# A fused cross-attention and quantised feed-forward kernel: the last up maximum by bank, first tiles in halves, even conversions two ahead

## The reference, cut to what matters

```python
def act_qdq(x):                       # 16 bits, one scale for the whole tensor
    scale = jnp.maximum(jnp.max(jnp.abs(x)) / 32767, 1e-12)
    return jnp.clip(jnp.round(x / scale), -32768, 32767) * scale
x = act_qdq(layernorm(x))             # [4096, 512]
up = act_qdq(x @ dq(w_up).T)          # [4096, 1536]
gate = act_qdq(x @ dq(w_gate).T)
gate = act_qdq(gate * round16(sigmoid(gate)))
o = act_qdq(gate * up)
out = x_before + o @ dq(w_down).T
```

## Time and profile before

| what | us |
|---|---|
| three timed runs | 900.43, 903.13, 906.34 |
| median of them | 903.13 |
| the profiled execution | 902.4 |
| its span, first to last instruction | 900.6 |
| busy in the span: PE, DVE, ACT, POOL | 870.8, 653.0, 555.6, 157.6 |

### The profile page before, as it was taken

How to read it: one execution, slowest core, us unless ns; L and a number is a source line. 1 busy time by engine, 2 the same in 40 slices (tenths; PEclk the granted TensorE clock), 3 DMA queues, 4 the chain that set the end, 5 groups by cost and what they waited for, 6 DMA issues and landing times.

```text
span 900.6 us, 11808 instructions
## 1 busy us (share of the span) xinstructions
PE 870.8 (97%) x4164; PEld 431.1 (48%) x4164; DVE 653.0 (73%) x921; ACT 555.6 (62%) x665; POOL 157.6 (17%) x160
## 2 busy tenths in 40 slices
PE   7999879999999999999999989999799989999998
PEld 5877554444444444444444434444344434444443
DVE  4879884664346243279997859857999997999892
ACT  2478755563553454489997859753789975555430
POOL 0199930079101950000000000000000000000000
PEclk9999979999999999999999999999999999999999
DMA  9822318865369649884339993799998887989872
GB/s 349 327 94 96 140 47 280 224 197 199 140 231 297 207 161 292 316 323 162 132 145 325 365 347 139 258 402 376 363 378 267 276 306 269 381 299 397 318 297 101
DMA packets 107549, 230.22 MB, mean 256 GB/s; under 512 B 47216, under 2 KB 47216, under 8 KB 105328
## 3 DMA queue, kind: packets, MB, share of 16 engines
q1 hardware_dynamic: 106352, 225.48, 70.6%
q10 hardware_dynamic: 1152, 4.19, 1.2%
HBM read 127.40 MB, written 92.27 MB: 244 GB/s over the span
## 4 chain that ended last, share of the span: by engine, by line
PE 73%; issue 12%; POOL 7%; DVE 3%; DMA 3%; SPq 1%; ACT 1%; POOLq 0%; ACTq 0%; DVEq 0%
PE ps L870 28%; PE ps L902 26%; PE ps L947 14%; PE ps L974 3%; DMA big<-in_L_ffn_w_gate_dram 2%; POOL big L705 2%; POOL big L694 1%; POOL big L688 1%; PE ps L964 1%; DVE small L1362 1%; POOL big L690 1%; POOL big L692 1%; DMA big<-gate_park 1%; POOL small L669 1%; SPq L388 1%
## 5 line engine op out<-in xcount | busy, mean ns | idle before, releaser
L992 ACT ACTIVATE big<-ps 128x1024 f32<-128x1024 f32 (+2 forms) x166 | 138.9, 845 | 194.3 <-PE ps L870 101.9
L902 PE MATMUL ps<-big 128*128 (+1 forms) x1152 | 249.0, 379 | 2.4 <-ACT big L992 2.4
L870 PE MATMUL ps<-big 128*128 (+1 forms) x1152 | 248.8, 379 | 1.6 <-DVE big L1445 1.6
L902 PEld LDWEIGHTS ps<-big 128*128 128x128 f16 x1152 | 112.7, 98 | 138.6 <-issue 2.9
L870 PEld LDWEIGHTS ps<-big 128*128 128x128 f16 x1152 | 112.6, 98 | 137.5 <-issue 1.8
L1463 DVE TENSOR_REDUCE small<-big 128x1 f32<-128x1024 f32 x48 | 58.4, 1220 | 133.9 <-ACT big L992 133.8
L947 PE MATMUL ps<-big 128*128 128x512 f16 x576 | 126.5, 382 | 2.4 <-DVE big L1602 2.4
L680 POOL PARTITION_ALL_REDUCE small<-small x8 | 3.3, 412 | 510.8 <-DVE small L1543 181.3
L947 PEld LDWEIGHTS ps<-big 128*128 128x128 f16 x576 | 56.6, 98 | 71.8 <-issue 5.1
L928 PE MATMUL ps<-big 128*128 128x512 f16 x384 | 85.3, 384 | 4.5 <-ACT big L1203 4.5
L1514 DVE CUSTOM_DVE_ANT_0 big<-big,small 128x1024 f32<-128x1024 int16 x48 | 61.7, 1285 | 7.0 <-DVE small L1508 0.2
(11 more groups left out here) (99 smaller groups left out, 1015.6 us busy)
## 6 DMA issues: line engine op xcount, KB each, us to landing
big<-up_park SPq DMA_DIRECT2D x90, 512.0 KB, 6.2
up_park<-big SPq DMA_DIRECT2D x48, 512.0 KB, 4.1
gate_park<-big SPq DMA_DIRECT2D x42, 512.0 KB, 2.9
big<-gate_park SPq DMA_DIRECT2D x42, 512.0 KB, 6.1
sign_park<-big SPq DMA_DIRECT2D x48, 256.0 KB, 3.0
big<-in_x_dram SPq DMA_DIRECT2D x8, 1024.0 KB, 18.1
x_park<-big SPq DMA_DIRECT2D x8, 1024.0 KB, 3.9
product_park<-big SPq DMA_DIRECT2D x16, 512.0 KB, 6.0
```

The lines of the kernel that those rows point to most:

```text
L870: mm = nc.tensor.matmul(ps[:, 2 * (n % 2) + j], w[:, a, k, o:o + P], XT[:, g, b, k], start=(k == 0 and a + b == 0), stop=(k == KC - 1 and ...
L902: mm = nc.tensor.matmul(ps[:, b + j], WU[:, a, k, o:o + P], XT[:, g, c, k], start=(k == 0 and a + c == 0), stop=(k == KC - 1 and c == 1))
L992: return nc.scalar.activation(dst, src, ACT.Copy)
```

## The change

- `up_max(47)` takes the maximum of the last up tile in two instructions, straight from PSUM, one for each bank: PE gives `u_mm` once more after the first bank (so its last count is NU + 1), and the two write the columns 48 and 0 of a `ucol` that is one column longer. ACT copies that tile out only after them (`take_up` waits for `u_mx` NU + 1). SP's wait for the last unit counts to NU + 1. The last two groups of the up product are written out instead of being the last turn of the loop.
- The search: tile 0 goes in halves of 512 columns on ACT, DVE (product only), ACT again and PE. The two late `give_sign` come behind the half products. `up_int(c)` for even c is issued a step earlier, so ACT's step is up_int(2t+4), up_int(2t+1), product_hi(t+1), and then `take_d1` as before. DVE's step is product(t+1), whole maximum(t), maximum of product(t). `slot_free` is rewritten for this order: the maximum of split tile 2t is now counted behind that of whole tile 2t+1.
- The down product: tile 0 goes in halves through `whole_int`, `down_hi`, `whole_lo` and PE; `split_int(0)` comes behind `whole_lo(0)`.
- Ring loads use the eight semaphores `c_ld` on; `it_ld` goes.

```diff
+        def int_given(eng, c):
+            eng.wait_ge(ra_d, (c + 1 if c < 4 else c) if c % 2 == 0 else min(c + 4, c // 2 + 26))
+
+        def product_given(eng, t):
+            eng.wait_ge(pr_d, t + 2)
+
+        def high_given(eng, t):
+            eng.wait_ge(ph_d, t + 2)
+
         def slot_free(eng, c):
-            eng.wait_ge(o_mx, c + 1)
-            if c % 2 == 0:
-                eng.wait_ge(ph_d, c // 2 + 1)
+            if c % 2:
+                eng.wait_ge(o_mx, c)
+            else:
+                eng.wait_ge(o_mx, c + 2)
+                high_given(eng, c // 2)
...
-            sp.wait_ge(u_mm, NU)
+            sp.wait_ge(u_mm, NU + 1)
...
-                sp.dma_start(ring(m), up_d[tile]).then_inc(it_ld[m % RING], 16)
+                l = len(LOADS) + m
+                sp.wait_ge(c_ld[l % 8], 16 * (l // 8))
+                sp.dma_start(ring(m), up_d[tile]).then_inc(c_ld[l % 8], 16)
...
-            def raise_unit(g, n):
+            def raise_unit(g, n, last=False):
                 b = 2 * ((n + 2) % 4)
                 for j in range(2):
+                    if last and j:
+                        mm.then_inc(u_mm, 1)
...
-            with nc.tensor.Fori(1, NG // 2) as t:
+            with nc.tensor.Fori(1, NG // 2 - 1) as t:
                 for n in range(2 * UPG):
                     pe.wait_ge(u_ev, 2 * UPG * t + n - 3)
                     raise_unit(2 * t + n // UPG, n)
+            for n in range(NU - 2 * UPG, NU):
+                pe.wait_ge(u_ev, n - 3)
+                raise_unit(n // UPG, n, n + 1 == NU)
...
-                    pe.wait_ge(ph_d, t + 1)
+                    if t == 0:
+                        for c in range(2):
+                            pe.wait_ge(ph_d, c + 1)
+                            for i in range(TI):
+                                for b in range(2):
+                                    nc.tensor.matmul(ps[:, b0 + i], halves[:, PART[t], c * 512 + i * P:c * 512 + i * P + P],
+                                                     WD[:, b, 2 * n + c], start=(c + b == 0), stop=False)
+                        continue
+                    high_given(pe, t)
...
-                    pe.wait_ge(ohi_d, q + 1)
-                    pe.wait_ge(olo_d, q + 1)
+                    if q == 0:
+                        for c in range(2):
+                            pe.wait_ge(ohi_d, c + 1)
+                            pe.wait_ge(olo_d, c + 1)
+                            for i in range(TI):
+                                at = slice(c * 512 + i * P, c * 512 + i * P + P)
+                                for a, b in ((0, 0), (0, 1), (1, 0)):
+                                    o = Qf[:, HALF[whole(q)], at] if a else hi_place(q)[:, at]
+                                    mm = nc.tensor.matmul(ps[:, i], o, WD[:, b, c], start=(c + a + b == 0), stop=False)
+                        mm.then_inc(first_mm, 1)
+                        continue
+                    pe.wait_ge(ohi_d, q + 2)
+                    pe.wait_ge(olo_d, q + 2)
...
-                act.wait_ge(u_mm, n + 1)
+                if n + 1 == NU:
+                    act.wait_ge(u_mx, NU + 1)
+                act.wait_ge(u_mm, NU + 1 if n + 1 == NU else n + 1)
...
-                need(act, o_mx, c - 3)
+                if c >= 4 and c % 2:
+                    act.wait_ge(o_mx, c - 4)
+                elif c >= 4:
+                    product_given(act, c // 2 - 2)
...
-            up_int(0)
+            for c in range(2):
+                w = slice(c * 512, c * 512 + 512)
+                nc.scalar.activation(r_int[:, 0, w], seat(0)[:, w], ACT.Copy, scale=col["uinv"]).then_inc(ra_d, 1)
+            up_int(2)
+            for c in range(2):
+                w = slice(c * 512, c * 512 + 512)
+                act.wait_ge(pr_d, c + 1)
+                nc.scalar.activation(halves[:, PART[0], w], seat(0)[:, w], ACT.Copy, scale=D1_SCALE).then_inc(ph_d, 1)
             for t in range(NS):
+                if t + 2 < NS:
+                    up_int(2 * t + 4)
                 up_int(2 * t + 1)
                 if t + 1 < NS:
-                    up_int(2 * t + 2)
-                product_hi(t)
+                    product_hi(t + 1)
                 if t >= 8 and t % UPG in (2, 4):
                     take_d1(2 * ((t - 8) // UPG) + t % UPG // 2 - 1)
...
+                l = len(LOADS) + m
+                act.wait_ge(c_ld[l % 8], 16 * (l // 8) + 16)
+                if m < 4 and m % 2:
+                    act.wait_ge(o_mx, NU - 4 + m)
+                elif m < 4:
+                    product_given(act, NS - 2 + m // 2)
                 elif m % 2:
                     act.wait_ge(so_d, m // 2 - 1)
                 else:
-                    act.wait_ge(oq_d, m // 2 - 1)
+                    act.wait_ge(oq_d, m // 2)
                 nc.scalar.activation(r_int[:, m % 4], ring(m), ACT.Copy, scale=col["uinv"]).then_inc(uq_d, 1)
 
             def down_hi(q):
...
             for q in range(NS):
-                down_hi(q)
                 if q == 0:
+                    for c in range(2):
+                        w = slice(c * 512, c * 512 + 512)
+                        act.wait_ge(oq_d, c + 1)
+                        nc.scalar.activation(hi_place(0)[:, w], Q[:, HALF[whole(0)], w], ACT.Copy).then_inc(ohi_d, 1)
                     down_int(2)
+                else:
+                    down_hi(q)
                 for m in (2 * q + 3, 2 * q + 4):
...
             def up_max(n):
+                if n + 1 == NU:
+                    for j in range(2):
+                        dve.wait_ge(u_mm, NU + j)
+                        nc.vector.tensor_reduce(ucol[:, (NU, 0)[j]:(NU, 0)[j] + 1], ps[:, 2 * ((n + 2) % 4) + j], AX.X, ALU.max,
+                                                apply_absolute_value=True).then_inc(u_mx, 1)
+                    return
                 dve.wait_ge(u_ev, n + 1)
-                nc.vector.tensor_reduce(ucol[:, n:n + 1], up_place(n), AX.X, ALU.max,
+                nc.vector.tensor_reduce(ucol[:, n + 1:n + 2], up_place(n), AX.X, ALU.max,
                                         apply_absolute_value=True).then_inc(u_mx, 1)
 
...
+            def split_product(t):
+                at = seat(2 * t)
+                if split(t) >= STAY:
+                    held_stored(dve, split(t))
+                if t == LATE_SIGNS:
+                    dve.wait_ge(sgn_d, NS)
+                int_given(dve, 2 * t)
+                nc.vector.tensor_tensor(at, r_int[:, 2 * t % 4], Q[:, HALF[split(t)]], ALU.mult).then_inc(pr_d, 1)
+
+            def whole_max(t):
+                c = 2 * t + 1
+                s = t % 2
+                int_given(dve, c)
+                if t > 1:
+                    dve.wait_ge(o_mx, 2 * t - 3)
+                nc.vector.tensor_tensor_reduce(seat(c), r_int[:, c % 4], Q[:, HALF[whole(t)]], 1.0,
+                                               ocol[:, s:s + 1], ALU.mult, ALU.max, ocol[:, s:s + 1]).then_inc(o_mx, 1)
+
+            held_stored(dve, split(0))
+            dve.wait_ge(sgn_d, LATE_SIGNS)
+            for c in range(2):
+                w = slice(c * 512, c * 512 + 512)
+                dve.wait_ge(ra_d, c + 1)
+                nc.vector.tensor_tensor(seat(0)[:, w], r_int[:, 0, w], Q[:, HALF[split(0)], w], ALU.mult).then_inc(pr_d, 1)
             for t in range(LATE_SIGNS, NS):
                 give_sign(t)
             for t in range(NS):
-                at = seat(2 * t)
-                if split(t) >= STAY:
-                    held_stored(dve, split(t))
-                if t in (0, LATE_SIGNS):
-                    dve.wait_ge(sgn_d, NS if t else LATE_SIGNS)
-                dve.wait_ge(ra_d, 2 * t + 1)
-                nc.vector.tensor_tensor(at, r_int[:, 2 * t % 4], Q[:, HALF[split(t)]], ALU.mult).then_inc(pr_d, 1)
-                dve.wait_ge(pr_d, t + 1)
-                nc.vector.tensor_reduce(ocol[:, 2 + t:3 + t], at, AX.X, ALU.max, apply_absolute_value=True).then_inc(o_mx, 1)
-                c = 2 * t + 1
-                s = t % 2
-                dve.wait_ge(ra_d, c + 1)
-                need(dve, o_mx, c - 3)
-                nc.vector.tensor_tensor_reduce(seat(c), r_int[:, c % 4], Q[:, HALF[whole(t)]], 1.0,
-                                               ocol[:, s:s + 1], ALU.mult, ALU.max, ocol[:, s:s + 1]).then_inc(o_mx, 1)
+                if t + 1 < NS:
+                    split_product(t + 1)
+                whole_max(t)
+                product_given(dve, t)
+                nc.vector.tensor_reduce(ocol[:, 2 + t:3 + t], seat(2 * t), AX.X, ALU.max,
+                                        apply_absolute_value=True).then_inc(o_mx, 1)
...
+                if q == 0:
+                    for c in range(2):
+                        w = slice(c * 512, c * 512 + 512)
+                        nc.vector.scalar_tensor_tensor(Q[:, h, w], r_int[:, 0, w], col["oinv"], Q[:, h, w], ALU.mult,
+                                                       ALU.mult).then_inc(oq_d, 1)
```

(37 more changed lines are left out.)

## The result

The changed kernel takes 914.26 us (median of 4 runs, 911.62 to 917.98). The kernel before took 903.36 beside it (900.43 to 906.34). I had forecast 910.0 and 7.2 us. The range (902 to 915) held the time, with 0.7 us to spare at its top; the size was short by 3 to 4 us.

What follows compares the result with a forecast made beforehand. DVE's 3.59 us step was taken to set the search. Terms: 1.35 (scale) - 1.85 (step 0) + 2.5 (steps) - 10.3 (waits) + 1.1 (join) = -7.2, giving 909.6 profiled, 910.0 as median; range 902 to 915.

Steps and rivals of the forecast that it cites:

- ACT's place in the step: Search: ACT's slack falls from 1.57 to 0.21 us; first-pass copies of 1.46 make DVE wait 1.26 each.
- Rival 1: Search, ACT's list at the six copies: copies don't delay needed conversions and loads land in time; 899.5 us; chance 0.12.
- The loads: Search, up tile loads: tile 42 lands late, wait 1.35 us; tile 46 with a copy on top, wait 2.63.
- Rival 2: Search: copies delay DVE but loads don't, landing 3.2 us and below the slack; 906.9 us; chance 0.17.
- Rival 3: Loads landing 4.9 to 5.9 us: waits at tiles 40, 42, 46 and in the ring; 912.6 to 916.6; chance 0.18.
- The steady step: Search on DVE: step falls from 3.59 to 3.48 us with the product followed at 1.14; 23 steps win 2.5.
- rival 4: Search on DVE: the product keeps its 1.25 us, so the 2.5 is not won; 911.1 us; chance 0.10.
- The start of the search: Search, step 0: two signs stand bare behind the half products and 1.2 us of wait appear; loss 1.85.
- The last up maximum: End of the up product: two maxima by bank make the scale of up ready 1.35 us earlier (1.15 to 1.45).
- DVE is busy with earlier maxima until 632.74: End of the up product: DVE finishes earlier maxima at 632.74, then runs two bank maxima of 0.65 us, ending at 633.92.
- The halves at the join: Start of the down product: first tile in halves, PE starts earlier, second tile's load wait is covered; gain 1.1 us.
- this wait is covered now: Start of the down product: the second tile's former 2.33 us wait for a ring load no longer counts.

Runs made afterwards that it cites:

- e4_odd_first: Changed kernel with ACT's odd conversion, wanted by the next whole maximum, issued before the even one: 906.84 us against 902.96 for the kernel before.
- e5_max_first: Changed kernel with DVE taking the maximum of product t ahead of whole maximum t: 904.95 us against 903.16 for the kernel before.
- e7_double_copies: Changed kernel with each of the six first-pass sum copies during the search done twice: 919.39 us against 903.16 for the kernel before.
- e6_both: Changed kernel with odd conversion first on ACT and product's maximum before the whole maximum on DVE: 903.35 us against 903.16 for the kernel before.
- e12_order_only: Kernel before with the search's new order, both exchanges, late signs before the half products; no bank maxima or down halves: 900.56 us against 903.11.
- e2_search_only: Kernel before with only the search's new order and first tile in halves; old last up maximum and down start: 912.84 us against 902.96.
- e1_bank_only: Kernel before with only the last up maximum by bank and the last twelve up units written out: 903.12 us against 902.96.
- e8_short_loads: Changed kernel with loads of up tiles 42 and 46 cut to 64 of 1024 columns: 913.17 us against 903.16 for the kernel before.
- e10_bank_loop: Kernel before with bank maxima of the last up tile, the loop kept, every up unit signalling each bank: 902.67 us against 903.11.
- e9_unrolled_only: Kernel before with only the last twelve up units written out: 903.31 us against 903.11.
- the last pair: Both exchanges without bank maxima, 902.49 us; then also without down halves and with late signs before the half products, 900.56; kernel before 903.11.

## Why the prediction was right, and where it was short

**ACT's place in the step: right, by its own numbers.** The slack of 0.21 at a copy that takes 1.46 gave waits of 1.26 on paper and 1.21 to 1.24 on the chip, at the maxima named. Rival 1 (ACT finds room) is out: adding to the copies adds as much to the waits, and adding slack from either side (`e4_odd_first`, `e5_max_first`) takes most of them away while the copies stay.

**The loads: right in kind, the sum a little high.** 1.35 and 2.63 were written, 1.38 and 2.24 measured. Shortening the two loads takes 0.6 and 1.3 of it away, where I had counted 1.35 and 1.37 on the loads. At 21 the failing piece is the adding: copy (1.26) and load run side by side, and `e7_double_copies` shows it. Rival 2 (no wait for loads) is out by the first number. Rival 3 (later loads) had three parts. At tiles 42 and 46 the waits are those of my own case, and no wait appeared at 40; but its ring loads did come late (5.5 and 6.7 us to landing, see below), and the measured 914.26 lies in its 912.6 to 916.6. The time alone would have spoken for it; the waits in the search don't.

**The steady step: right.** 3.47 against 3.48. The product is followed after 1.25 us where the next operation reads it and after 1.13 where it doesn't. That is not the kind of the next operation: in `e6_both` a maximum follows the product as in the earlier trace rows, but it reads the product before, and it starts after 1.13 too (649.65 to 650.78). So rival 4 is out. The rule of the Trainium skill that stood behind it ("VectorE: DVE Perf Modes", section "The DRAIN you can't avoid") was measured there on copies and does not hold for this pair: the traces put 0.12 us on each product, some 2.8 us over 23 steps. This is also what `e12_order_only` keeps.

**The start of the search: right.** The signs stood bare behind the half products and the first whole maximum waited 1.04, forecast 1.2. Together with the three terms above the search was forecast 9.7 longer and was 9.4 (`e2_search_only`: 98.7 us from join to join, 9.5).

**The last up maximum: wrong, the term "1.35 (scale)".** The step that failed is "DVE is busy with earlier maxima until 632.74": I took DVE as free at the last matmul's end, from one execution in which it was so by 0.2 us. In the traces of after and of all six kernels with bank maxima by the written-out units (`e1_bank_only`, `e4_odd_first` to `e8_short_loads`) DVE was at earlier work until 0.1 to 3.6 us past that end, and in `e10_bank_loop` until 2.8. Where DVE was all but free, the edit did its work: in `e4_odd_first` it was late by 0.1 us, and the join stands 1.3 us behind the last matmul in place of 2.3. Timed, the edit alone gave +1.3 us with the written-out units and -1.0 without by the ratios, neither told from nothing. I had worked out when the banks were complete but not how far DVE's queue could be behind. Why it is further behind in these kernels than in most of the others is open. In the trace of after, a load of signs landed late (DVE waited 5.26 us for it; in the trace of before, 4.28 at the same place) and the maxima queued up behind the signs. That the edit causes this isn't shown: `e9_unrolled_only`, without bank maxima, has 1.5 us of it, the five other kernels without them at most 0.2.

**The halves at the join: wrong, the term "+1.1 (halves and load wait at the join)".** The step that failed is "this wait is covered now". PE does start early, 4.06 us after the join in place of 5.33, but the second tile counts, and its conversions wait for ring loads. The forecast had 3.7 us from issue to landing for the late up tiles and "no wait" for the ring; the two ring loads that ACT waited for in after took 5.5 and 6.7. The second tile was to start 11.0 us after the search's last maximum; it started 11.8 after it, and 12.0 before the change. So 0.2 of the 1.1 came. In the kernels with halves the second `whole_lo` starts 10.5 to 11.0 us after the join, in those without 9.9 to 11.2, and from the join to the end the first take 175.3 to 175.9 us, the second 174.8 to 176.2: the traces show neither a gain nor a cost of the halves. By the times there may be a small cost: alone they measured +1.4 us by the ratio, with an interval that starts at 0.1, and leaving them out in the last pair goes the same way (902.49 to 900.56, but there the signs were moved too, and the traces give 0.7 us of it to the search, 87.5 to 86.7, and none to the down product). It isn't shown.

**The sum.** With these two terms at nothing the working gives 7.2 + 1.35 + 1.1 = 9.7, and 10.3 [7.9, 12.7] was measured. The forecast's size was short by two gains counted as won; its mechanism stood. That the time still fell in the range is in part luck: its top had been set for late loads, not for these two terms. The first line of the table, 3.4 us of the profiled difference, can't be put down to the change. In the up stage PE waits once for a copy, and how long differs from one execution to the next:

```profile
540.37 96.01 PE L916 MATMUL ps<-big 128*128 x432 [4.41 <-ACT big L1026]
```

That is after. Before it stood there with the same 432 matmuls:

```profile
539.55 93.41 PE L902 MATMUL ps<-big 128*128 x432 [2.41 <-ACT big L992]
```

A gap 2.0 us longer (it also began earlier), and 2.6 more for the same matmuls. The 2.6 is PE's clock behind the gap: in after it stood at 0.50, in before at 1.00 (columns as above).

```profile
540.40:543.00 2.60, 2.60 (x7) 0.95 (x8) 2.46 (x5) 2.51 (x3) 0.00 (x0) 0.50 0.52 213
```

```profile
539.60:542.20 2.60, 2.60 (x13) 1.19 (x14) 2.46 (x5) 2.51 (x3) 0.00 (x0) 1.00 0.55 221
```

`e6_both`, which has all of the change's edits to the up product, shows 1.98 and 93.41 as before does; `e12_order_only`, which has none of them, shows 3.82 and 95.10. So it goes with the execution and not with the edit. The medians of the timed runs contain it on both sides.

## What to carry to other kernels

When one engine's order is shifted by a step, write down for each in-order list how long after its release an operation is done, and how long after it is wanted. Then set the slack against what comes only now and then (here six copies in 24 steps), not against the mean load. On a list that serves two consumers, the operation wanted first goes first: that one exchange was worth 6 us here. And an engine that is "just free" in one profile is not free; a gain that needs it free at a moment wants several executions behind it.

## What was not expected of the hardware

PE's clock after the idle stretch before the down product does not follow the stretch's length. The next lines are the windows of after and of `e12_order_only` at the first down tile (with PE alone: window, its length, PE busy, granted clock, DMA share, GB/s), then PE's own line of `e4_odd_first` and of `e6_both`.

```profile
742.40:745.00 2.60, 2.60 (x7) 0.50 0.96 329
```

```profile
728.83:731.30 2.47, 2.47 (x12) 1.00 1.00 401
```

```profile
731.19 7.03 PE L973 MATMUL ps<-big 128*128 128x512 f16 x24 [3.22 <-ACT big L1297]
```

```profile
726.99 5.34 PE L971 MATMUL ps<-big 128*128 128x512 f16 x24 [3.21 <-ACT big L1295]
```

After 5.39 us idle the granted clock was 0.50 (1.2 GHz), and the first tile's 24 matmuls took 7.65 us. After 2.41 in the kernel before it was 0.50 too, and after 3.22 in `e4_odd_first` the tile took 7.03. But after 2.73 in `e12_order_only` it stayed at 1.00 (2.4 GHz), and there and after 3.21 in `e6_both` the tile took 5.34. The kernel before shows both by itself: idle for 2.41 us in the up product it stood at 1.00 behind the gap, idle for 2.41 before the down product at 0.50. What decides isn't shown. I had counted on half a clock after every gap of this size. In after it costs nothing: the first tile ends at 750.00 and the operands of the second are complete at 749.92. Where the operands come earlier it does, as in `e10_bank_loop` beside `e9_unrolled_only`: 1.4 us to the end.
